# Experts' gate and up chunks of a decoder layer: seven block products per pair in place of eight

## What is computed

```python
# x: 4096 normed tokens; 16 experts, 2 per token, capacity C = 640 tokens; F = 704
def _mlp(h, wg, wu, wd):
    return jax.nn.silu(h @ wg) * (h @ wu) @ wd
...
logits = x_tokens @ router_w + router_b
vals, idx = top_k(softmax(logits), 2)
expert_inputs = jnp.zeros((E, C, d)).at[idx_flat, pos_c].add(x_pair)
expert_outputs = jax.vmap(_mlp)(expert_inputs, w_gate, w_up, w_down)
...
return x + _mlp(x, sw_gate, sw_up, sw_down) + output_tokens
```

## Time and profile before

| | |
|---|---|
| Median of three runs | 1820.36 us (1820.07 to 1820.89) |
| Span of the profiled execution | 1818.3 us (first to last instruction; the median of the runs lies 2.1 above) |
| PE busy | 1804.8 us (99%), 9977 matmul records |
| DVE, ACT, POOL busy | 873.3, 800.0, 922.2 us |
| An expert | 58.0 us |

### The profile page before, as it was taken

The page is one execution under the profiler, slowest core; times in us unless marked ns, Lnnn a source line. Parts: engine busy times, 40 slices in busy tenths (PEclk is TensorE's granted clock), DMA queues, the critical chain, the costliest instruction groups (busy, mean ns, idle before and its releaser), DMA issues.

```text
span 1818.3 us, 27202 instructions
## 1 busy us (share of the span) xinstructions
PE 1804.8 (99%) x9977; PEld 1598.7 (88%) x9977; DVE 873.3 (48%) x2067; ACT 800.0 (44%) x1574; POOL 922.2 (51%) x809
## 2 busy tenths in 40 slices
PE   9999999999999999999999999999999999999997
PEld 6888888888887878888999999999999999999997
DVE  6668777787745444332444324343334423443242
ACT  4555556555544343332444434444344434444331
POOL 3454464546653232225665656556665566656632
PEclk9999999999999999999999999999999999999999
DMA  8454555453552333225676676666666766667722
GB/s 319 147 134 122 151 140 150 134 143 95 147 116 40 47 52 68 37 42 103 161 141 132 163 156 134 135 150 158 147 140 126 164 149 140 145 138 163 145 41 29
DMA packets 254436, 229.35 MB, mean 126 GB/s; under 512 B 171712, under 2 KB 171968, under 8 KB 253024
## 3 DMA queue, kind: packets, MB, share of 16 engines
q1 hardware_dynamic: 228864, 174.51, 36.7%
q0 software_dynamic: 25440, 53.11, 17.3%
HBM read 138.80 MB, written 49.97 MB: 104 GB/s over the span
## 4 chain that ended last, share of the span: by engine, by line
PE 94%; DVE 2%; DMA 1%; issue 1%; POOL 1%; ACT 1%; SPq 0%; POOLq 0%; DVEq 0%; ACTq 0%
PE ps L72 66%; PE ps L1692 23%; PE ps L1002 3%; PE ps L1146 1%; PE ps L1008 0%; DMA buffer<-means 0%; ACT buffer L528 0%; DMA buffer<-in_x 0%; POOL buffer L481 0%; DMA means<-mean 0%; DVE buffer L832 0%; DVE stats L736 0%; DMA tokens_normed<-buffer 0%; ACT buffer L1491 0%; DMA buffer<-buffer 0%
## 5 line engine op out<-in xcount | busy, mean ns | idle before, releaser
L72 PE MATMUL ps<-buffer,buffer 128*128 128x320 f32 (+1 forms) x6900 | 1239.1, 341 | 1.3 <-DVE buffer L832 0.8
L72 PEld LDWEIGHTS ps<-buffer,buffer 128*128 128x128 f32 x6900 | 1121.0, 188 | 107.5 <-issue 1.5
L1426 POOL TENSOR_TENSOR buffer<-buffer,buffer 128x512 fp32r<-128x512 f32 x289 | 380.4, 1480 | 251.6 <-ACT buffer L1491 251.1
L1692 PE MATMUL ps<-buffer,buffer 128*128 128x512 f32 (+1 forms) x1921 | 437.6, 388 | 0.4 <-DVE buffer L1624 0.4
L1692 PEld LDWEIGHTS ps<-buffer,buffer 128*128 128x128 f32 x1921 | 356.9, 188 | 73.9 <-issue 1.2
L1533 ACT ACTIVATE buffer<-ps 128x320 f32<-128x320 f32 (+1 forms) x240 | 112.5, 469 | 599.6 <-PE ps L72 594.0
L1491 ACT ACTIVATE buffer<-buffer 128x512 fp32r<-128x512 f32 (+1 forms) x491 | 293.4, 652 | 163.4 <-PE ps L1692 90.6
L1599 DVE TENSOR_TENSOR ps<-ps,buffer 128x320 f32<-128x320 f32 (+2 forms) x198 | 100.2, 506 | 487.5 <-ACT buffer L1533 477.0
L1480 POOL DMA_INDIRECT out_tokens<-buffer,slot_list x79 | 124.0, 1569 | 185.5 <-DVE buffer L1636 177.3
L520 POOL DMA_INDIRECT slots<-pairs,slot_u x64 | 63.6, 994 | 181.8 <-DVE slot_u L989 164.8
L528 ACT ACTIVATE buffer<-buffer 128x512 fp32r<-128x512 f32 (+1 forms) x212 | 127.0, 683 | 19.9 <-DMA buffer<-buffer 15.2
(11 more groups left out here) (134 smaller groups left out, 1094.0 us busy)
## 6 DMA issues: line engine op xcount, KB each, us to landing
buffer<-in_wts SPq DMA_DIRECT2D x289, 256.0 KB
buffer<-in_xT SPq DMA_DIRECT2D x8, 1024.0 KB, 5.5
buffer<-in_ctxT SPq DMA_DIRECT2D x8, 1024.0 KB, 8.2
out_tokens<-buffer SPq DMA_DIRECT2D x8, 1024.0 KB, 4.3
tokens_normed<-buffer SPq DMA_DIRECT2D x32, 256.0 KB, 3.1
out_tokens<-buffer POOLq DMA_DIRECT2D x32, 256.0 KB, 5.1
buffer<-in_x SPq DMA_DIRECT2D x7, 1024.0 KB, 5.5
buffer<-combiners_top SPq DMA_DIRECT2D x6, 1024.0 KB, 4.9
```

The lines of the kernel that those rows point to most:

```text
L72: last = pe.matmul(out, left, right, start=(c == 0 and i == 0), stop=(c == len(parts) - 1 and i == 2))
L1426: pool.tensor_tensor(wl[n % RING][:], wraw[n % RAW][:], wh[n % RING][:].bitcast(F32), ALU.subtract).then_inc(s_wl, 1)
L1692: ins = pe.matmul(down_bank[(n + i) % 2][:, part_cols], left, right, start=(c == 0 and k == 0), stop=(c == FC - 1 and k == len(passes) - 1))
```

## The change

It applies the seven-product scheme for 2x2 blocks to each pair of a gate and an up chunk. The blocks of the weights are gate and up (rows) by first and second half of the 512 features; the blocks of the tokens are the halves of the features by the two halves of the tokens. Seven products of 6 matmuls each replace eight. Four sums of weight blocks and four of token blocks are formed first (DVE), each again split into high and low part; the results are put together on DVE from four banks (`ps[0]`, `ps[1]` and two of four cross banks). The mixed chunk and down are computed as before.

- Weights: a pair of chunks now becomes seven blocks of 128x256, high and low (`high_parts`, `high_sums` on ACT, `weight_sums` on DVE, `low_parts` on POOL), in four slots; the other seven chunks have eight slots. `prepared` says after which step each is made.
- Tokens: the five tiles' words are put together on ACT alone (`words`), in an order by halves of tiles; `token_sums`, `token_sum_hi` and `token_sum_lo` are new. Words and the sums' high parts share rows, so they are written after the last pair's products (`words_free`).
- Gathered tokens `xn` share rows with `ost`, so a gather waits for the adds of two groups before, and the first scaling for the transposes.
- Products lie in SBUF (`up0`, `up1`), no longer in PSUM.
- The shared expert's groups are as before, except that the first expert's tokens and weights are prepared in the last of them.

The core of the diff:

```diff
-    RING = 22
-    TURN_AT = RAW + 4
+    PAIRS = FC - 1
+    SINGLES = WC - 2 * PAIRS
+    PAIR_SLOTS, SINGLE_SLOTS = 4, 8
+    PER_PAIR = 7
+    HALF, TH = CAP // 2, P // 2
+    TOKEN_PARTS = [(0, 2), (2, 4), (4, 5)]
...
+    cross_bank = [(ps[2], ps[3]), (ps[6], ps[7])]
...
-    xh, xl, xw = at(52, [NC, CAP], F32R), at(84, [NC, CAP], F32R), at(84, [NC, CAP])
+    xw, xh, xl = at(57, [2, NC, HALF]), at(52, [2, NC, HALF], F32R), at(84, [2, NC, HALF], F32R)
+    tw, th, tl = at(94, [4, 2, HALF]), at(57, [4, 2, HALF], F32R), at(94, [4, 2, HALF], F32R)
...
+    xn = at(89, [ET, 2 * D], U16)
...
+    prepared = {(3, 1): [("pair", 0)], (B - 1, 2): [("pair", 1)], (B - 1, 4): [("pair", 2)], (B - 1, "down0"): [("pair", 3)]}
+    for e in range(E):
+        q, m = e * PAIRS, e * SINGLES
+        prepared[B + e, 1] = [("pair", q + 4)]
+        prepared[B + e, 2] = [("single", m + i) for i in range(4)]
+        prepared[B + e, 3] = [("single", m + i) for i in range(4, SINGLES)]
+        if e + 1 < E:
+            prepared[B + e, 4] = [("pair", q + PAIRS)]
+            prepared[B + e, 5] = [("pair", q + PAIRS + 1)]
+            prepared[B + e, "down1"] = [("pair", q + PAIRS + 2)]
+            prepared[B + e, "down3"] = [("pair", q + PAIRS + 3)]
...
+        def low_parts(kind, i):
+            if kind == "single":
+                n, k = single_chunk(i), single_slot(i)
...
+            n, k, done = pair_chunk(i), pair_slot(i), parts_before_pair(i)
+            hi, lo = pair_hi[k], pair_lo[k]
+            pool.wait_ge(s_hi, done + 1)
+            pool.tensor_tensor(lo[:, 0:2].rearrange("p b c f -> p (b c f)"), wraw[n % RAW][:],
+                               hi[:, 0:2].bitcast(F32).rearrange("p b c f -> p (b c f)"), ALU.subtract).then_inc(s_lo, 1)
+            pool.wait_ge(s_hi, done + 2)
+            pool.tensor_tensor(lo[:, 2].rearrange("p c f -> p (c f)"), wraw[(n + 1) % RAW][:, D // 2:D],
+                               hi[:, 2].bitcast(F32).rearrange("p c f -> p (c f)"), ALU.subtract).then_inc(s_lo, 1)
+            pool.wait_ge(s_hi, done + 3)
+            pool.tensor_tensor(lo[:, 3:7].rearrange("p b c f -> p (b c f)"),
+                               pair_sum[k][:].rearrange("p b c f -> p (b c f)"),
+                               hi[:, 3:7].bitcast(F32).rearrange("p b c f -> p (b c f)"), ALU.subtract).then_inc(s_lo, 1)
...
+        def high_sums(kind, i):
+            if kind == "pair":
+                k = pair_slot(i)
+                act.wait_ge(s_sum, 4 * (i + 1))
+                copy(pair_hi[k][:, 3:7].rearrange("p b c f -> p (b c f)"),
+                     pair_sum[k][:].rearrange("p b c f -> p (b c f)")).then_inc(s_hi, 1)
...
+        def words(e, t):
+
+            if t == 0:
+                act.wait_ge(s_xp, 16 * ET * (e + 1))
+                words_free(act, e)
+            copy(word_halves_of(t)[:, :, :, :, 1], turned_words(t, slice(0, NC))).then_inc(s_xraw, 1)
+            copy(word_halves_of(t)[:, :, :, :, 0], turned_words(t, slice(NC, 2 * NC))).then_inc(s_xraw, 1)
...
+        def pair_products(e, p):
+            g, q = B + e, e * PAIRS + p
+            u = unit_no[(g, p, 0)]
+            act.wait_ge(s_prod, PER_PAIR * q + 1)
+            if q > 0:
+                act.wait_ge(s_comb, 5 * (q - 1) + 2)
+            copy(kept[:], ps[0][:, 0:HALF]).then_inc(s_keep, 1)
+            if p > 0:
+                h_hi(e, p - 1, 0)
+                h_hi(e, p - 1, 1)
+            act.wait_ge(s_prod, PER_PAIR * q + 2)
+            if u - SHARED_UNITS >= 4:
+                act.wait_ge(s_hl, u - 2)
+            copy(up1[p % 2][:], cross_bank[p % 2][0][:, 0:HALF]).then_inc(s_keep, 1)
+            prepare(g, p, second=False)
+            act.wait_ge(s_prod, PER_PAIR * q + 4)
+            if q > 0:
+                act.wait_ge(s_ht, u - 1)
+            act.activation(silu0[:], ps[0][:, 0:HALF], ACT.Silu).then_inc(s_silu, 1)
+            prepare(g, p, first=False)
+            act.wait_ge(s_comb, 5 * q + 4)
+            act.activation(gate1[:], gate1[:], ACT.Silu).then_inc(s_silu, 1)
...
+        for e in range(E):
+            g = B + e
+            for p in range(PAIRS):
+                pair_products(e, p)
+            c = FC - 1
+            h_hi(e, c - 1, 0)
+            h_hi(e, c - 1, 1)
+            if e + 1 < E:
+                words(e + 1, 0)
+            for j, place in enumerate((silu0, gate1)):
+                act.wait_ge(s_mix, 2 * e + j + 1)
+                act.wait_ge(s_ht, unit_no[(g, c - 1, j)] + 1)
+                act.activation(place[0:FH, :], cross_bank[c % 2][j][0:FH, 0:HALF], ACT.Silu).then_inc(s_silu, 1)
+            for j in range(2):
+                h_hi(e, c, j)
+            prepare(g, c)
+            if e + 1 < E:
+                words(e + 1, 1)
+                token_hi(e + 1, 0)
+                words(e + 1, 2)
+                words(e + 1, 3)
+                token_hi(e + 1, 1)
+                token_sum_hi(e + 1, 0)
+                prepare(g, "down1")
+                words(e + 1, 4)
+                token_hi(e + 1, 2)
+                token_sum_hi(e + 1, 1)
+                token_sum_hi(e + 1, 2)
+                prepare(g, "down3")
 
...
+        def weight_sums(kind, i):
...
+            dve.tensor_tensor(s3, gate[:, 0:half], up[:, 0:half], ALU.subtract).then_inc(s_sum, 1)
+            dve.tensor_tensor(s1, up[:, 0:half], up[:, half:D], ALU.add).then_inc(s_sum, 1)
+            dve.wait_ge(s_sum, 4 * i + 1)
+            dve.tensor_tensor(s2, up[:, half:D], s3, ALU.subtract).then_inc(s_sum, 1)
+            dve.wait_ge(s_sum, 4 * i + 3)
+            dve.tensor_tensor(s4, gate[:, half:D], s2, ALU.subtract).then_inc(s_sum, 1)
...
+            dve.tensor_tensor(t1, b12, b11, ALU.subtract).then_inc(s_tsum, 1)
+            dve.tensor_tensor(t3, b22, b12, ALU.subtract).then_inc(s_tsum, 1)
+            dve.wait_ge(s_tsum, 4 * n + 1)
+            dve.tensor_tensor(t2, b22, t1, ALU.subtract).then_inc(s_tsum, 1)
+            dve.wait_ge(s_tsum, 4 * n + 3)
+            dve.tensor_tensor(t4, b21, t2, ALU.subtract).then_inc(s_tsum, 1)
...
+        def h_lo(e, c, j):
+            rows = slice(0, rows_of(c))
+            lo = half_columns(hl, rows, c, j) if c < FC - 1 else half_columns(hh, slice(FH, P), c, j)
+            product = up0 if j == 0 else up1[c % 2]
+            dve.wait_ge(s_hh, unit_no[(B + e, c, j)] + 1)
+            dve.tensor_tensor(lo, by_tile(product[rows, :]), half_columns(hh, rows, c, j).bitcast(F32),
+                              ALU.subtract).then_inc(s_hl, 1)
...
+        def pair_combined(e, p):
+            g, q = B + e, e * PAIRS + p
+            u = unit_no[(g, p, 0)]
+            second, fourth = (bank[:, 0:HALF] for bank in cross_bank[p % 2])
+            up_1 = up1[p % 2][:]
+            if p > 0:
+                h_lo(e, p - 1, 0)
+                h_lo(e, p - 1, 1)
+            dve.wait_ge(s_prod, PER_PAIR * q + 3)
+            dve.wait_ge(s_keep, 2 * q + 2)
+            dve.tensor_tensor(up_1, fourth, up_1, ALU.add).then_inc(s_comb, 1)
+            prepare(g, p)
+            dve.wait_ge(s_prod, PER_PAIR * q + 5)
+            dve.wait_ge(s_comb, 5 * q)
+            dve.tensor_tensor(base[:], ps[1][:, 0:HALF], kept[:], ALU.add).then_inc(s_comb, 1)
+            dve.wait_ge(s_comb, 5 * q + 2)
+            dve.tensor_tensor(up_1, base[:], up_1, ALU.add).then_inc(s_comb, 1)
+            dve.wait_ge(s_prod, PER_PAIR * q + 6)
+            dve.wait_ge(s_ht, u)
+            dve.tensor_tensor(gate1[:], second, base[:], ALU.add).then_inc(s_comb, 1)
+            dve.wait_ge(s_prod, PER_PAIR * q + 7)
+            dve.wait_ge(s_hl, u)
+            dve.tensor_tensor(up0[:], fourth, base[:], ALU.add).then_inc(s_comb, 1)
+            dve.wait_ge(s_comb, 5 * q + 5)
+            dve.wait_ge(s_silu, u + 1)
+            dve.tensor_tensor(up0[:], up0[:], silu0[:], ALU.mult).then_inc(s_ht, 1)
+            dve.wait_ge(s_silu, u + 2)
+            dve.tensor_tensor(up_1, up_1, gate1[:], ALU.mult).then_inc(s_ht, 1)
...
+            token_sums(e + 1, 0)
+            token_lo(e + 1, 0)
+            scaled(g, 0)
+            token_sums(e + 1, 1)
+            token_lo(e + 1, 1)
+            token_sum_lo(e + 1, 0)
+            scaled(g, 1)
+            prepare(g, "down1")
+            token_sums(e + 1, 2)
+            token_lo(e + 1, 2)
+            scaled(g, 2)
+            token_sum_lo(e + 1, 1)
+            token_sum_lo(e + 1, 2)
+            prepare(g, "down3")
+            scaled(g, 3)
+            scaled(g, 4)
...
+        def product(bank, hi, lo, x_hi, x_lo, first):
+            for c in range(2):
+                passes = [(hi[:, c], x_hi[:, c]), (hi[:, c], x_lo[:, c]), (lo[:, c], x_hi[:, c])]
+                for i, (left, right) in enumerate(passes):
+                    ins = pe.matmul(bank[:, 0:HALF], left, right, start=(first and c == 0 and i == 0),
+                                    stop=(c == 1 and i == 2), skip_group_check=not first)
+            ins.then_inc(s_prod, 1)
+
```

(52 more changed lines are left out.)

593 lines of the change are left out of this document (362 added, 231 removed).

## The result

The changed kernel takes 2091.07 us (median of four runs, 2089.87 to 2092.69) beside 1820.62 for the one before: ratio 1.1489, 95% interval 1.1472 to 1.1505. The forecast was 2003 in a range of 1900 to 2090. The sign held, the size fell short by 88 us, and the result lies 1 us outside the range.

The account below looks back on a forecast made before the run. PE, busy 99%, bounded the kernel; turns between DVE and POOL would make it wait. Fifteen experts +177, last -2, expert 0 +8: span 1818.3 + 183 = 2001, plus 2.1 for the median: 2003 us, range 1900 to 2090.

Parts of the forecast that it names:

- PE's saving and the prices: Experts' gate and up: 30 fewer matmuls each, 4.4 us saved, five pairs 30.8; wide forms 1.2 DVE, 1.06 ACT, 2.5 POOL.
- The tail without turns: Mixed chunk and down, no DVE-POOL exclusion: PE waits 5.5 us, expert 59.2; order-alone rival 1840 us, chance 0.06.
- The tail with turns: Mixed chunk and down, DVE two-SBUF-input instructions and POOL's TENSOR_TENSORs excluding each other: 36.6 us, waits 3.4, 5.7, 0.4, 4.2.
- The ends: First and last experts: expert 0 delayed by 8 us, last expert, without tail work, 2 us shorter.
- The step that failed: Fourth pair: each adjacent DVE two-input instruction waits for one full POOL subtraction (1.1 us), so PE waits 2.4 us.
- The clock rival: PE's clock falls to 1.2 GHz after long waits: up to 7.7 us per expert, 2060 to 2115 us; chance 0.12.
- PE stays the bound: Experts: POOL's subtractions fall into DVE's waits, PE waits under 4.25 us; 1750 to some 1785 us; chance 0.10.
- The signs named: Six experts over 400 us; PE waits name L1871, L1816 first; listed DVE lines well over 0.5 us, L1829, L1833 at 0.5.

Follow-up runs that it names:

- run 6: The change with gate, up and their products formed in place in PSUM cross banks instead of SBUF: 1963 us.
- run 14: The change with products in PSUM, scalings first, weight preparation spread, and POOL waiting for a step's weight sums before its subtractions: 1900 us.
- run 4: The change with POOL's subtractions for the experts' weights replaced by filling their outputs with zeros: 1840 us.
- run 5: The change with POOL waiting, behind its gather, for a DVE instruction of the third pair before going on with its subtractions: 2060 us.
- run 2: The change with POOL waiting for DVE's L1835 before the first single low part of the third and fourth pairs: 2055 us.
- runs 3 and 12: The change with filler matmuls ahead of PE's three long waits, 2092 us; the change with POOL's gap behind the gather and fillers in the tail, 2057 us.
- run 13: The change with expert weights' low parts zero-filled, scalings first and weight preparation spread over the expert: 1781 us.
- run 7: The change with DVE's scalings 0 to 3 placed before the token sums of the same step: 2039 us.
- run 8: The change with expert weights' low parts zero-filled and scalings placed before the token sums: 1813 us.
- runs 11 and 14: The change with products in PSUM, scalings first and weight preparation spread, 1984 us; the same with POOL waiting for a step's weight sums, 1900 us.
- run 10: The change with weight preparation spread over the expert, one pair instead of three left in the tail: 2115 us.
- run 9: The change with products formed in PSUM and scalings placed before the token sums: 1971 us.

## Why the prediction was right and wrong

**PE's saving and the prices** held: 30.8 us for five pairs where nothing waits (run 6), and means of 1218 ns for a 128x1024 on DVE (1.2), 1056 on ACT (1.06), 2598 with turns and 2.39 us alone on POOL (2.5). POOL's 128x256 took 1078 with turns and 0.74 us alone (run 14), where 0.65 was assumed.

**The tail without turns** (59.2 an expert, 1840 us) held in run 4, which measured 59.2 and 1840. **The tail with turns** (36.6) held at 36.2, though in part by luck: the sixth chunk waited 1.7 and not 3.4, scaling 1 not at all, scaling 2 2.9 and not 4.2, while the clock added 2.8. Scalings were forecast to end at 20.3, 24.6 and 32.7; they ended at 18.7, 23.1 and 32.1.

**The ends** held: expert 0 began 9.2 us late (889.54 for 880.39; +8 forecast), the last expert was 2.0 shorter (65.9 for 67.8; -2 forecast). The fifteen others took 75.5 and not 69.8: 5.7 x 15 = 86 of the 88 us.

**The step that failed** is in the walk of the pairs: "each adjacent DVE two-input instruction waits a full POOL one (1.1)", from which "PE waits 2.4". In the rows that I had the earlier trace rows, DVE got in after each subtraction, and I took that for a rule. Here one addition waited for five, and PE waited 5.3: 2.9 us more. Behind that wait the clock fell, another 2.8. Run 5 shows both that the subtractions themselves do not force it and what remains when it is gone: PE waits of 0.6 and 1.4 and a pair stage of 34.8, near the 33.2, but a tail of 37.6. It gives back only 31 of the 88 us (run 2: 36). An expert still takes 73.3 on the mean and not 69.8, since of the 4.1 us that the pair stage gains the tail gives back 1.4; so the step explains the form of the miss in the change, but taken alone not its whole size. Which turn in the tail takes the rest, no run here separates.

**The clock rival** was half right. The clock does fall, to 0.50 behind each wait of over 5 us, down tiles included, which was the sign named for it; so its chance of 0.12 was too low as to whether it happens. The Trainium skill (TensorE: Matmul & The Clock Gate, "HAM oscillation — how this bites in real kernels") says that such gaps lower it, and the trace agrees. The waits of 1.84 us in run 4 are shorter than the gaps that the section speaks of, and the clock fell behind some of them; there the measurement decides. But its price, up to 7.7 us an expert, did not stand in the change: runs 3 and 12 restored the clock and got back 0.6 to 1.2 us an expert. DVE and POOL set the tail, and a faster PE waits longer. Its time, 2060 to 2115, holds the measured 2091 by luck.

**"PE stays the bound"** came true in no version with the real subtractions. With them gone and the order mended it comes nearly true (run 13), which says what the rival lacked. Neither by itself decides the sign: without the turns but in the old order the time is 1840 (run 4), with the turns and the scalings first 2039 (run 7), with both mended 1813 (run 8). The sums of busy time showed neither.

**The signs named** were met in part. Six experts took 450 us (over 400 was named) and L1829 and L1833 stayed at 0.49. PE's waits named L1871 first, but `kept` second and L1816 only third; and of the lines that were to average well over 0.5, L1783 (1.61), L1844 (0.86) and L1764 (0.77) did, L1846 (0.58), L1766 (0.54) and L1768 (0.43) hardly or not. The turns were not spread over all lines; a few long ones made much of the time (L1835, not on that list: 1.80 on the mean, 7.4 at most).

## What to carry to other kernels

Before you give DVE work with two SBUF inputs, list what POOL does at the same time, and count not one subtraction but the whole run that can stand ready, above all behind a gather or scatter of POOL's own. Keep operands in PSUM where a bank is free, or make POOL wait for the DVE step that the path needs: the 84 us between runs 11 and 14 came from idling an engine. A saving of 8% of the busiest engine's time in an expert can't be counted until its feeders' chain is walked with their contention.

## What was not expected of the hardware

DVE's turn depends on how POOL's run began. In runs of subtractions that POOL began after a real wait, a DVE instruction with two SBUF inputs got in at the next border (run 5: 16 of 16 at each of the two borders named). In runs begun right behind POOL's indirect DMAs it was mostly passed over: at four borders in a row in the change (7.39 us for 0.49), at six in run 10 (9.43 us); at the first border behind the gather it did get in. Cutting the wide subtraction in two added a border and no entry. Why that is, no run here shows; that a gap of some 4 us ahead of the run (62.9 us in 16 times) ends it, run 5 does. The change's own trace has both kinds beside each other: in runs that POOL began after a wait, DVE got in at all 56 borders at which such an instruction stood ready; at the border from L1516 to L1519 behind the scatter of the tail it was passed over 15 of 15 times.

The granted clock fell to 0.50 behind waits of 5.3 and 5.4 us, and not behind the 2.9 us in the same expert. But the length of a wait alone does not tell: in run 4 it fell behind 1.84 us in some experts and not in others, in run 9 behind waits of 0.4 to 2.4 close together.
